# Weighting the experts' rows in their slots and adding them to the residual in the gather itself

## The chip, the cores and the metric

The kernel runs on one core of one Trainium2 chip. The metric is the device time of one execution in microseconds, the median of several runs. A profiled execution also has a span: the time from its first to its last recorded event.

## The reference

The reference is one decoder layer over 8 x 256 = 2048 tokens of width 512: retention, then cross-attention, then a feed-forward with eight experts, each added to a residual. The change lies in the feed-forward alone, in fp32:

```python
xf = layernorm(x)                                   # 2048 x 512
probs = softmax(xf @ gate_w.T)                      # 8 experts
top_p, top_i = top_k(probs, 2)                      # each token goes to two experts
out_e = (silu(xf @ fc1[e].T) * (xf @ fc2[e].T)) @ proj[e].T     # hidden width 352
shared = (silu(xf @ s1.T) * (xf @ s2.T)) @ sproj.T              # hidden width 1408
x = x + top_p[0] * out_e[top_i[0]] + top_p[1] * out_e[top_i[1]] + sigmoid(xf @ sg.T) * shared
```

## The kernel before

The residual `X` stays in SBUF as 16 tiles (`NT`) of 128 tokens by 512 columns. Matrix products are made of three passes over high and low halves of fp32 values (`matmul3`), so TensorE has the most work.

The feed-forward runs in stages. The shared expert goes first, in `STEPS` = 44 steps: 11 pieces of the hidden width, each over 4 groups (`G`) of 512 tokens. Its last eight steps are only half done there; their hidden values are held, and their down products follow at the very end (`held_down`). Meanwhile DVE works out the router: `gain[:, k, t]` is a token's weight for its first (`k` = 0) or second (`k` = 1) expert, `rows[:, k, t]` the row that it has in a table in DRAM. Tokens are sorted by expert into 39 slots (`SLOTS`) of 128 rows. Of a token's two rows, `k` = 0 is the one of the expert with the lower number, so no such row belongs to the last expert.

GpSimd (POOL) writes each token's normalized row to its two places of `rows_in` (`scatter`, 32 indirect DMAs, between its halves of pieces 3 to 6), splits the weights of the shared expert (`split`, pieces up to 10) and of the experts (`fetch` and `expert`).

Then TensorE works through the 39 slots. For each one SP loads 128 rows, TensorE transposes them, multiplies up, transposes the hidden values and multiplies down; ACT copies the product from PSUM to `ye` (`product_out`, three buffers); SP stores `ye` to `rows_out`. Each engine works through its list in the order written.

The end, which the change is about:

- POOL gathers 16 tiles of `k` = 0 rows into `early`, as soon as the last expert but one is through (semaphore `ye_done`); at most three are in flight (`landed0`). Then it waits until all `ye` stores have landed (ACT adds 3 to `ye_done` for this) and gathers 16 tiles of `k` = 1 rows into `late`.
- TensorE runs `held_down(0)` to `held_down(3)`: four sums of 128 x 512 each into PSUM. `held_down(2)` and `(3)` wait until DVE has added the sums of two groups before (`dadded`), whose PSUM banks they reuse. `held_down(3)` also needs two last pairs of hidden values split by ACT and DVE (`pair_high` and `pair_low`, 6 and 7).
- DVE does, in this order: 16 sums with `early` (`expert_sum(t, 0)`), `pair_low(6)` and `(7)`, 16 additions of the shared expert (`dadded`), 16 sums with `late` (`expert_sum(t, 1)`).
- SP stores tile `t` of the residual to the output when `expert_sum(t, 1)` is done.

Of the kernel before, what the change touches and what calls it, by code (L numbers as in the profile page):

```python
# [6 lines left out]
FP32 = mybir.dt.float32  # L7
# [4 lines left out]
ALU = mybir.AluOpType  # L12
# [3 lines left out]
P = 128  # L16
# [64 lines left out]
def retention(nc, X, slots, first, table, x_dram, wa_dram, decay_dram, rot_dram, gn_dram, blk_dram, ident, ident_dram,  # L81
# [4 lines left out]
    with ExitStack() as mem:  # L86
# [86 lines left out]
        def _(sp):  # L173
# [24 lines left out]
            for which in range(2):  # L198
                for g in range(B):
                    sp.dma_start(pack_dram[g, which, 3 * XD:3 * XD + 2, :, :, :].rearrange("r h c (a s) -> (r h c a) s", a=TB),  # L200
                                 fix[:, which, :]).then_inc(fix_out, 16)
            for n in range(SLOTS):
                for rows in row_tables:
                    sp.dma_start(rows[n * P:(n + 1) * P, :], zero_dram).then_inc(filled, 16)
# [13 lines left out]
            sp.wait_ge(fix_out, 32 * B)  # L218
            sp.wait_ge(filled, 32 * SLOTS)

# [1396 lines left out]
def feed_forward(nc, X, final, row_tables, lead, ws_dram, we_dram, ident, out_dram):  # L1617
# [12 lines left out]

    rows_in, rows_out = row_tables
    with ExitStack() as mem:
        def sb(name, shape, dt=FP32, stack=mem):
            return stack.enter_context(nc.sbuf_tensor("c_" + name, shape, dt))

        def pb(name, shape, stack=mem):
            return stack.enter_context(nc.psum_tensor("c_" + name, shape, FP32))
# [7 lines left out]
        with ExitStack() as view:  # L1645
            eraw = sb("eraw", [P, RING, 2 * EW], FP32, view)
        with ExitStack() as view:
            sb("below", [P, 2 * EW], FP32, view)
            late = sb("late", [P, NT, C], FP32, view)
            sb("between", [P, 2 * EW - NT * C], FP32, view)  # L1650
            early = sb("early", [P, NT, C], FP32, view)
        ring = sb("ring", [P, RING * 2 * EW], FP32R)
# [25 lines left out]
        gain = sb("gain", [P, 2, NT])  # L1678
        rows = sb("rows", [P, 2, NT], I32)
        tiles_e, upto, base = sb("tiles_e", [P, E]), sb("upto", [P, E]), sb("base", [P, E])  # L1680
        words = sb("words", [P, 5])
# [3 lines left out]
        with ExitStack() as view:  # L1685
            tp, rl = pb("tp", [P, 2, C], view), pb("rl", [P, C], view)
        with ExitStack() as view:
            eh, ey = pb("eh", [P, C], view), pb("ey", [P, 2, C], view)
# [25 lines left out]
        ye_out = [sem("ye_out%d" % k) for k in range(3)]  # L1714
        landed0, landed1 = [sem("landed0%d" % k) for k in range(3)], [sem("landed1%d" % g) for g in range(G)]
        ph_done, pl_done, pm_done, dm_done, dadded = (sem(k) for k in ("ph_done", "pl_done", "pm_done", "dm_done", "dadded"))
        summed, freed = sem("summed"), sem("ring_freed")
        block = mem.enter_context(nc.Block())
# [22 lines left out]
        def rows_at(n):  # L1741
            return xe[:, n % 4, :]

        def tile_of(idx):
            return 4 * (idx // 4 % G) + idx % 4

        @block.sync
        def _(sp):
# [11 lines left out]
            for f in range(3, HID):  # L1760
                piece(f)
            sp.wait_ge(scattered, 16 * 2 * NT)
            sp.wait_ge(ymm_done, 4 * G * 9)
            for n in range(6):
# [6 lines left out]
            for t in range(NT):  # L1771
                sp.wait_ge(summed, NT + t + 1)
                sp.dma_start(out_dram[:, t, :], X[:, t, :]).then_inc(stored, 16)
# [3 lines left out]
        def _(pool):  # L1777
# [26 lines left out]

            def gather(t, k, into):
                nc.gpsimd.indirect_dma_start(  # L1806
                    out=into[:, t, :], out_offset=None, in_=rows_out,
                    in_offset=bass.IndirectOffsetOnAxis(ap=rows[:, k, t:t + 1], axis=0)).then_inc(landed1[t // 4] if k else landed0[t % 3], 16)

# [17 lines left out]
            for f in range(7, HID):  # L1827
                split(f)
            expert(0)
            pool.wait_ge(fc_done, STEPS)  # L1830
# [14 lines left out]
            for t in range(NT):  # L1845
                if t >= 3:
                    pool.wait_ge(landed0[t % 3], 16 * (t // 3))
                gather(t, 0, early)
            pool.wait_ge(ye_done, SLOTS + 3)
            for t in range(NT):  # L1850
                gather(t, 1, late)

        @block.vector
        def _(dve):
# [187 lines left out]
            for n in range(SLOTS):  # L2042
# [5 lines left out]
                if 2 <= n < 8:  # L2048
                    pair_low(n - 2)
            def expert_sum(t, k):  # L2050
                if k:
                    dve.wait_ge(landed1[t // 4], 64)
                    dve.wait_ge(dadded, t + 1)
                else:
                    dve.wait_ge(landed0[t % 3], 16 * (t // 3 + 1))
                nc.vector.scalar_tensor_tensor(out=X[:, t, :], in0=(early, late)[k][:, t, :], scalar=gain[:, k, t:t + 1],
                                               in1=X[:, t, :], op0=ALU.mult, op1=ALU.add).then_inc(summed, 1)

            for t in range(NT):
                expert_sum(t, 0)  # L2060
            pair_low(6)
            pair_low(7)
            for g in range(G):
                for k in range(4):
                    t = 4 * g + k
                    dve.wait_ge(dm_done, t + 1)
                    dve.wait_ge(summed, t + 1)
                    nc.vector.scalar_tensor_tensor(out=X[:, t, :], in0=sum_at(g, k), scalar=shared[:, t:t + 1],
                                                   in1=X[:, t, :], op0=ALU.mult, op1=ALU.add).then_inc(dadded, 1)
            for t in range(NT):  # L2070
                expert_sum(t, 1)

        @block.scalar
        def _(act):
# [50 lines left out]
            def product_out(n):  # L2125
                act.wait_ge(d_done, n + 2)
                if n >= 3:
                    act.wait_ge(ye_out[n % 3], 16 * (n // 3))
                nc.scalar.copy(ye[:, n % 3, :], ey[:, n % 2, :]).then_inc(ye_done, 1)

# [33 lines left out]
            high_xT(1)  # L2164
            act.wait_ge(hf_done, STEPS)
            expert_silu(0)
            for n in range(SLOTS):
                high_hT(n)
                if n + 1 < SLOTS:
                    expert_silu(n + 1)  # L2170
                if n + 2 < SLOTS:
                    high_xT(n + 2)
                product_out(n)
                if 2 <= n < 8:
                    pair_high(n - 2)
# [7 lines left out]
        def _(pe):  # L2183
# [248 lines left out]
def decoder_layer(nc, ins, out_dram):  # L2432

    with ExitStack() as mem:
        X = mem.enter_context(nc.sbuf_tensor("residual", [P, NT, C], FP32))
        ident = mem.enter_context(nc.sbuf_tensor("identity", [P, P], FP32))
        tables = [nc.dram_tensor("c_rows_" + k, (SLOTS * P, C), FP32).ap() for k in ("in", "out")]
        final = [mem.enter_context(nc.sbuf_tensor("final_" + k, [P, NT], FP32)) for k in ("mean", "var", "rstd")]
# [30 lines left out]
```

## Time and profile before

| | us |
|---|---|
| time, median of 3 runs (1445.61 to 1447.66) | 1446.95 |
| time of the profiled execution | 1445.69 |
| its span | 1443.9 |
| TensorE busy (matmul) | 1332.0 |
| DVE busy | 850.2 |
| GpSimd busy | 515.6 |
| ScalarE busy | 483.9 |

The profiled execution is 1.3 us below the median, and its time is 1.8 us above its span. A busy share is a mean over the whole span; the last 40 us look quite different from the rest, and the change has to be read there.

### The profile page before, as it was taken

What the parts mean: (1) busy time and instruction counts of PE and PEld (TensorE: products, weight loads), DVE (VectorE), ACT (ScalarE), POOL (GpSimd) and SP (SyncE); (2) the same over time, 40 slices, a digit from 0 to 9 for tenths busy, and PEclk for the clock granted to TensorE, in tenths of its full rate; (3) what the DMA queues carried; (4) which work ended last, traced back from release to release, by engine and by line L of the source; (5) the groups of instructions that cost most, each with busy time, mean ns of one, the idle gap of its engine ahead of it and who ended that gap; (6) DMA issues with size and microseconds to landing.
All of it is one profiled execution on the core that took longest, in us unless ns stands there. A gap on an engine that the chain in (4) does not pass through costs nothing. (4 is left out here: it accounts for less than half of the span.)

```text
span 1443.9 us, 24104 instructions
## 1 busy us (share of the span) xinstructions
PE 1332.0 (92%) x8442; PEld 1071.4 (74%) x8442; DVE 850.2 (59%) x1516; ACT 483.9 (34%) x756; POOL 515.6 (36%) x353
## 2 busy tenths in 40 slices
PE   6899999998489999999889999999999999999994
PEld 5577777776366667666557788888887889999983
DVE  5666667675588887788763557556554243222247
ACT  4122222224156556565574311111110233223220
POOL 1122212215354333343142006542133375574045
PEclk9999999999789999999999999999999999999998
DMA  7991000000465445544600002330000434334256
GB/s 252 329 330 59 0 0 0 0 1 23 148 180 164 145 144 156 164 138 143 180 19 22 1 22 99 138 147 22 22 23 30 161 127 151 136 137 149 74 161 232
DMA packets 84891, 159.83 MB, mean 111 GB/s; under 512 B 8560, under 2 KB 61936, under 8 KB 81392
## 3 DMA queue, kind: packets, MB, share of 16 engines
q1 hardware_dynamic: 78544, 124.19, 27.3%
q0 software_dynamic: 6272, 34.61, 6.6%
q8 instruction: 51, 0.84, 0.2%
q14 instruction: 24, 0.20, 0.0%
HBM read 109.22 MB, written 69.47 MB: 124 GB/s over the span
## 5 line engine op out<-in xcount | busy, mean ns | idle before, releaser
L1278 DVE TENSOR_REDUCE b_mx<-b_rt 128x4 f32<-128x1024 f32 x128 | 156.3, 1221 | 51.4 <-PE b_rt L1100 51.3
L1435 ACT ACTIVATE b_pf<-b_rt,b_zero 128x1024 f32<-128x1024 f32 x128 | 142.8, 1116 | 126.7 <-PE b_rt L1112 126.4
L1961 DVE SCALAR_TENSOR_TENSOR residual<-c_yp,c_shared,residual 128x512 f32<-128x512 f32 x144 | 103.8, 744 | 113.6 <-PE c_yp L43 113.6
L41 PE MATMUL c_fc<-c_xh,c_w 128*128 128x512 f32 x352 | 137.7, 391 | 0.0
L43 PE MATMUL c_fc<-c_xh,c_w 128*128 128x512 f32 x352 | 137.1, 389 | 0.0
L42 PE MATMUL c_fc<-c_xl,c_w 128*128 128x512 f32 x352 | 137.0, 389 | 0.0
L41 PE MATMUL c_fc<-c_ring,c_xTl 128*128 x312 | 105.8, 339 | 0.0
L2099 ACT ACTIVATE c_s<-c_fc 128x512 f32<-128x512 f32 x44 | 26.3, 598 | 232.0 <-PE c_fc L43 231.9
L43 PE MATMUL c_fc<-c_ring,c_xTh 128*128 x312 | 100.8, 323 | 0.0
L42 PE MATMUL c_fc<-c_ring,c_xTh 128*128 x312 | 100.6, 322 | 0.0
L1781 POOL TENSOR_TENSOR c_w<-c_wraw,c_zero 128x1536 fp32r<-128x1536 f32 x9 | 24.8, 2751 | 202.5 <-DMA c_wraw<-in_c_ws 108.5
L1975 DVE TENSOR_TENSOR c_hTl<-c_eh,c_hTh 128x384 fp32r<-128x384 f32 x39 | 21.7, 557 | 120.0 <-ACT c_hTh L2123 120.0
L1100 PE MATMUL b_rt<-weights_b 50*128 50x256 f32 x512 | 66.5, 339 | 26.5 <-DVE b_mx L1278 19.7
L1100 PEld LDWEIGHTS b_rt<-weights_b 50*128 50x128 f32 x512 | 39.7, 191 | 60.1 <-DVE b_mx L1278 31.9
L1801 POOL TENSOR_TENSOR c_ring<-c_eraw,c_zero 128x2816 fp32r<-128x2816 f32 (+1 forms) x16 | 62.8, 3926 | 53.2 <-DMA c_eraw<-in_c_we 53.2
L1803 POOL TENSOR_TENSOR c_ring<-c_eraw,c_ring 128x2816 fp32r<-128x2816 f32 (+1 forms) x16 | 78.8, 4926 | 1.3
L43 PEld LDWEIGHTS c_fc<-c_xh,c_w 128*128 128x128 f32 x352 | 66.1, 188 | 13.9
L41 PEld LDWEIGHTS c_fc<-c_xh,c_w 128*128 128x128 f32 x352 | 66.1, 188 | 13.5
L42 PEld LDWEIGHTS c_fc<-c_xl,c_w 128*128 128x128 f32 x352 | 66.1, 188 | 13.3
L1125 PE MATMUL b_av<-b_pf,b_vp 128*32 128x256 f32 x1024 | 69.2, 388 | 0.0
L41 PE MATMUL a_gemm<-weights_a,a_xl 128*128 128x512 f32 x128 | 56.2, 439 | 9.2 <-DVE a_xl L455 9.2
L41 PEld LDWEIGHTS c_fc<-c_ring,c_xTl 128*128 128x128 f32 x312 | 59.0, 189 | 7.4 <-issue 6.7
(386 smaller groups left out, 3499.3 us busy)
## 6 DMA issues: line engine op xcount, KB each, us to landing
weights_b<-b_pack SPq DMA_DIRECT2D x128, 200.0 KB
c_eraw<-in_c_we POOLq DMA_DIRECT2D x8, 2176.0 KB, 9.6
b_pack<-b_hi SPq DMA_DIRECT2D x56, 256.0 KB, 2.5
c_rows_in<-in_b_ctx SPq DMA_DIRECT2D x39, 256.0 KB, 9.9
c_rows_out<-in_b_ctx SPq DMA_DIRECT2D x39, 256.0 KB, 10.0
c_xe<-c_rows_in SPq DMA_DIRECT2D x39, 256.0 KB, 3.0
c_rows_out<-c_ye SPq DMA_DIRECT2D x39, 256.0 KB, 2.0
c_wraw<-in_c_ws SPq DMA_DIRECT2D x11, 768.0 KB, 4.4
```

Of the source, the lines that this page charges most:

```text
L41: nc.tensor.matmul(out, ll, rh, start=start, stop=False)
L42: nc.tensor.matmul(out, lh, rl, start=False, stop=False)
L43: return nc.tensor.matmul(out, lh, rh, start=False, stop=stop)
L1100: last = nc.tensor.matmul(rt[:, e, t * S:(t + 1) * S], qT[r, p, t * P:(t + 1) * P], kT[r, p, :], start=True, stop=True)
L1125: last = nc.tensor.matmul(av[r:r + VW, 0:S], vp[:, j * XH + h, :], pf[:, h % 8, j * S:(j + 1) * S], start=j == 0, stop=j == TB - 1)
L1278: nc.vector.tensor_reduce(out=mx[:, :, 2 * p:2 * p + 2].rearrange("p t e -> p e t"), in_=rt[:, 0:2, :].rearrange("p e (t s) -> p e t s", s ...
L1435: nc.scalar.activation(pf[:, s:s + 2, :], rt[:, 2:4, :], ACT.Exp, scale=XD ** -0.5, bias=zero[:, :]).then_inc(e_done, 1)
L1781: nc.gpsimd.tensor_tensor(w[k][:, 0, :], wraw[k][:, 1, :], zero[:, :].to_broadcast([P, PW]), ALU.add).then_inc(high_done, 1)
L1801: nc.gpsimd.tensor_tensor(high, raw, zero[:, :].to_broadcast([P, hi - lo]), ALU.add).then_inc(high_done, 1)
L1803: nc.gpsimd.tensor_tensor(low, raw, as_f32(high), ALU.subtract).then_inc(ew_done, 1)
L1961: nc.vector.scalar_tensor_tensor(out=X[:, t, :], in0=yp[:, (n * 4 + k) % 3, :], scalar=shared[:, t:t + 1], in1=X[:, t, :], op0=ALU.mult, o ...
L2099: nc.scalar.activation(s[:, n % 2, :], fc[:, n % 2, 0, :], ACT.Silu).then_inc(s_done, 1)
```

## The change

Each expert's rows are multiplied by their token's weight before they are stored, so that what lies in `rows_out` is already weighted. For this the weight has to be known by slot and row. POOL writes `gain` to a new table of one column in DRAM with the indices of the rows (`spread_weights`, 32 indirect DMAs of 128 x 4 bytes, eight after each of the pieces 7 to 10); SP reads the table back as 39 partitions of 128 weights; TensorE transposes it once, ahead of the slots; ACT copies it to SBUF; and `product_out` becomes an activation with a scale for each partition in place of a copy. The transposed weights and the table read back lie in tiles that are no longer used by then.

Both gathers then add their rows to `X` in the DMA (`compute_op=ALU.add`). The 32 sums on DVE and the tiles `early` and `late` are gone. A gather of `k` = 1 into tile `t` waits until DVE has added the shared expert's part of that tile, and that addition waits for the landing of the gather of `k` = 0. SP stores tile `t` when its `k` = 1 gather has landed: the first twelve in groups of four, the last four one by one.

```diff
+            sp.dma_start(row_tables[2].rearrange("(n p) o -> n (p o)", p=P), zero_dram[0:SLOTS, 0:P]).then_inc(filled, 16)
...
+        by_slot = hit[0:SLOTS, :, :].rearrange("p t e -> p (t e)")
+        weight_at = prob[:, :, :].rearrange("p t e -> p (t e)")[:, 0:SLOTS]
...
+        def landing(t):
+            return (landed1[t // 4], 64) if t < NT - 4 else (landed1[G - 1 + t - (NT - 4)], 16)
...
             sp.wait_ge(scattered, 16 * 2 * NT)
+            sp.wait_ge(spread, 16 * 2 * NT)
+            sp.dma_start(by_slot, weights_dram.rearrange("(n p) o -> n (p o)", p=P)).then_inc(weights_in, 16)
             sp.wait_ge(ymm_done, 4 * G * 9)
...
             for t in range(NT):
-                sp.wait_ge(summed, NT + t + 1)
+                sp.wait_ge(*landing(t))
                 sp.dma_start(out_dram[:, t, :], X[:, t, :]).then_inc(stored, 16)
...
+            def spread_weights(t):
+                for k in range(2):
+                    nc.gpsimd.indirect_dma_start(
+                        out=weights_dram, out_offset=bass.IndirectOffsetOnAxis(ap=rows[:, k, t:t + 1], axis=0),
+                        in_=gain[:, k, t:t + 1], in_offset=None).then_inc(spread, 16)
+
+            def gather_add(t, k):
                 nc.gpsimd.indirect_dma_start(
-                    out=into[:, t, :], out_offset=None, in_=rows_out,
-                    in_offset=bass.IndirectOffsetOnAxis(ap=rows[:, k, t:t + 1], axis=0)).then_inc(landed1[t // 4] if k else landed0[t % 3], 16)
+                    out=X[:, t, :], out_offset=None, in_=rows_out,
+                    in_offset=bass.IndirectOffsetOnAxis(ap=rows[:, k, t:t + 1], axis=0),
+                    compute_op=ALU.add).then_inc(landing(t)[0] if k else landed0[t % 3], 16)
...
             for f in range(7, HID):
                 split(f)
+                for t in range(4 * (f - 7), 4 * (f - 6)):
+                    spread_weights(t)
...
             for t in range(NT):
-                gather(t, 1, late)
+                pool.wait_ge(dadded, t + 1)
+                gather_add(t, 1)
...
-            for t in range(NT):
-                expert_sum(t, 0)
-            pair_low(6)
-            pair_low(7)
             for g in range(G):
                 for k in range(4):
                     t = 4 * g + k
                     dve.wait_ge(dm_done, t + 1)
-                    dve.wait_ge(summed, t + 1)
+                    dve.wait_ge(landed0[t % 3], 16 * (t // 3 + 1))
                     nc.vector.scalar_tensor_tensor(out=X[:, t, :], in0=sum_at(g, k), scalar=shared[:, t:t + 1],
                                                    in1=X[:, t, :], op0=ALU.mult, op1=ALU.add).then_inc(dadded, 1)
-            for t in range(NT):
-                expert_sum(t, 1)
+                if g == 0:
+                    pair_low(6)
+                    pair_low(7)
...
-                nc.scalar.copy(ye[:, n % 3, :], ey[:, n % 2, :]).then_inc(ye_done, 1)
+                nc.scalar.activation(ye[:, n % 3, :], ey[:, n % 2, :], ACT.Identity, scale=weight_at[:, n:n + 1],
+                                     bias=zero[:, :]).then_inc(ye_done, 1)
...
             act.wait_ge(hf_done, STEPS)
+            act.wait_ge(turned_done, 1)
+            nc.scalar.copy(weight_at, turned[:, :]).then_inc(weights_done, 1)
             expert_silu(0)
+            act.wait_ge(weights_done, 1)
...
+            pe.wait_ge(weights_in, 16)
+            nc.tensor.transpose(turned[:, :], by_slot, ident[0:SLOTS, 0:SLOTS]).then_inc(turned_done, 1)
             transpose_rows(0)
```

## Rows read from the trace of the kernel before

**Rows 1.** The page, part 1: TensorE's busy time and share.
```profile
PE 1332.0 (92%) x8442; PEld 1071.4 (74%) x8442; DVE 850.2 (59%) x1516; ACT 483.9 (34%) x756; POOL 515.6 (36%) x353
```

**Rows 2.** The chain that ended last, from 1402 us: start us, us, what.
```profile
1402.66 0.60 ACT c_ye L2129
1403.28 2.73 DMA c_rows_out<-c_ye
...
1406.38 6.26 POOL c_late L1806
...
1430.92 6.41 DMA c_late<-c_rows_out,c_rows
```

**Rows 3.** Timeline of POOL: start us, us, instruction, idle time before and its releaser.
```profile
1380.11 1.04 POOL L1806 DMA_INDIRECT c_early<-c_rows_out,c_rows  x1 [53.95 <-ACT c_ye L2129]
...
1384.31 0.95 POOL L1806 DMA_INDIRECT c_early<-c_rows_out,c_rows  x1 [0.65 <-DMA c_early<-c_rows_out,c_rows]
...
1401.38 1.44 POOL L1806 DMA_INDIRECT c_early<-c_rows_out,c_rows  x1 [0.49 <-DMA c_early<-c_rows_out,c_rows]
1403.12 1.02 POOL L1806 DMA_INDIRECT c_early<-c_rows_out,c_rows  x1 [0.30 <-issue]
...
1412.94 0.94 POOL L1806 DMA_INDIRECT c_late<-c_rows_out,c_rows  x1 [0.30 <-issue]
...
1426.72 1.24 POOL L1806 DMA_INDIRECT c_late<-c_rows_out,c_rows  x1 [0.30 <-issue]
```

**Rows 4.** Timeline of DVE from 1399 us.
```profile
1399.90 10.71 DVE L2056 SCALAR_TENSOR_TENSOR residual<-c_early,c_gain,residual 128x512 f32<-128x512 f32 x16
...
1411.74 2.71 DVE L2068 SCALAR_TENSOR_TENSOR residual<-c_fc,c_shared,residual 128x512 f32<-128x512 f32 x4
...
1426.40 8.03 DVE L2056 SCALAR_TENSOR_TENSOR residual<-c_late,c_gain,residual 128x512 f32<-128x512 f32 x12
1437.35 2.74 DVE L2056 SCALAR_TENSOR_TENSOR residual<-c_late,c_gain,residual 128x512 f32<-128x512 f32 x4 [2.91 <-DMA c_late<-c_rows_out,c_rows]
```

**Rows 5.** Timeline of SP's DMA queue: the output's stores.
```profile
1427.17 13.48 SPq L1773 DMA_DIRECT2D out<-residual  x16
```

**Rows 6.** DMA, 1413 to 1427 us: GB/s by slices of 0.35 us, the queue, landings.
```profile
GB/s 12 211 257 234 129 140 269 222 141 152 257 222 141 187 293 164 117 234 281 164 222 222 222 164 316 222 164 129 304 211 140 140 328 211 140 234 211 164 234 293
...
q0 software_dynamic: 854, 2.84, 70.4%
...
c_late<-c_rows_out,c_rows POOLq DMA_INDIRECT x12, 3.7
```

**Rows 7.** DMA, 1427 to 1443.9 us: packets, MB, share of 16 engines.
```profile
q1 hardware_dynamic: 2304, 4.20, 64.5%
q0 software_dynamic: 426, 1.36, 24.5%
```

**Rows 8.** Groups of ACT, shapes apart: count, busy us, mean ns, idle before.
```profile
L2129 ACT COPY c_ye<-c_ey 128x512 f32<-128x512 f32 x39 | 22.9, 588 | 64.5 <-PE c_ey L43 64.5
...
L708 ACT ACTIVATE a_gcn<-a_rt,a_gb,a_ga 128x256 f32<-128x256 f32 x32 | 15.5, 565 | 30.3 <-DVE a_gb L562 30.3
L686 ACT COPY a_qk<-a_gemm 128x256 f32<-128x256 f32 x32 | 11.9, 373 | 128.6 <-PE a_gemm L43 128.6
```

**Rows 9.** POOL's other DMAs: duration min/median/max ns, first and last start us.
```profile
L1787 POOL DMA_INDIRECT c_rows_in<-c_xn,c_rows x32: 957/963/1432, 880.8 to 955.5; - x32
...
L1792 POOL DMA_DIRECT2D c_eraw<-in_c_we x8: 556/562/592, 958.5 to 1298.8; - x8
```

**Rows 10.** Timeline of POOL: the split of piece 10.
```profile
1073.19 3.51 POOL L1783 TENSOR_TENSOR c_w<-c_wraw,c_w 128x1536 fp32r<-128x1536 f32 x1
```

**Rows 11.** Timeline of SP's DMA queue: the first loads of slots' rows.
```profile
1100.20 35.63 SPq L1757 DMA_DIRECT2D c_xe<-c_rows_in  x6
```

**Rows 12.** Timeline of TensorE: matmuls of the held products.
```profile
1414.51 0.50 PE L41 MATMUL c_fc<-c_w,c_keep_low 128*128 128x512 f32 x1 [1.00 <-DVE residual L2068]
...
1425.31 0.39 PE L43 MATMUL c_ex<-c_w 128*128 128x512 f32 x1
```

More of the change, by code:

```diff
@@ L201, in _ @@
                                  fix[:, which, :]).then_inc(fix_out, 16)
+            sp.dma_start(row_tables[2].rearrange("(n p) o -> n (p o)", p=P), zero_dram[0:SLOTS, 0:P]).then_inc(filled, 16)
             for n in range(SLOTS):
-                for rows in row_tables:
+                for rows in row_tables[0:2]:
                     sp.dma_start(rows[n * P:(n + 1) * P, :], zero_dram).then_inc(filled, 16)
@@ L218, in _ @@
             sp.wait_ge(fix_out, 32 * B)
-            sp.wait_ge(filled, 32 * SLOTS)
+            sp.wait_ge(filled, 32 * SLOTS + 16)
         @block.tensor
@@ L1629, in feed_forward @@
     MAGIC = 1.5 * 2.0 ** 23
-    rows_in, rows_out = row_tables
+    rows_in, rows_out, weights_dram = row_tables
     with ExitStack() as mem:
@@ L1646, in feed_forward @@
             eraw = sb("eraw", [P, RING, 2 * EW], FP32, view)
[L1647 to L1651, printed above, removed]
         ring = sb("ring", [P, RING * 2 * EW], FP32R)
@@ L1686, in feed_forward @@
             tp, rl = pb("tp", [P, 2, C], view), pb("rl", [P, C], view)
+        with ExitStack() as view:
+            turned = pb("turned", [P, SLOTS], view)
         with ExitStack() as view:
@@ L1714, in feed_forward @@
         ye_out = [sem("ye_out%d" % k) for k in range(3)]
-        landed0, landed1 = [sem("landed0%d" % k) for k in range(3)], [sem("landed1%d" % g) for g in range(G)]
+        landed0, landed1 = [sem("landed0%d" % k) for k in range(3)], [sem("landed1%d" % g) for g in range(G + 3)]
         ph_done, pl_done, pm_done, dm_done, dadded = (sem(k) for k in ("ph_done", "pl_done", "pm_done", "dm_done", "dadded"))
-        summed, freed = sem("summed"), sem("ring_freed")
+        spread, weights_in, turned_done, weights_done = sem("spread"), sem("weights_in"), sem("turned_done"), sem("weights_done")
+        freed = sem("ring_freed")
         block = mem.enter_context(nc.Block())
@@ L1803, in expert @@
                     nc.gpsimd.tensor_tensor(low, raw, as_f32(high), ALU.subtract).then_inc(ew_done, 1)
-            def gather(t, k, into):
+            def spread_weights(t):
[4 more added lines that the diff above has]
+            def gather_add(t, k):
                 nc.gpsimd.indirect_dma_start(
-                    out=into[:, t, :], out_offset=None, in_=rows_out,
-                    in_offset=bass.IndirectOffsetOnAxis(ap=rows[:, k, t:t + 1], axis=0)).then_inc(landed1[t // 4] if k else landed0[t % 3], 16)
+                    out=X[:, t, :], out_offset=None, in_=rows_out,
+                    in_offset=bass.IndirectOffsetOnAxis(ap=rows[:, k, t:t + 1], axis=0),
+                    compute_op=ALU.add).then_inc(landing(t)[0] if k else landed0[t % 3], 16)
             nc.gpsimd.memset(zero[:, :], 0.0).then_inc(presets, 1)
@@ L1847, in _ @@
                     pool.wait_ge(landed0[t % 3], 16 * (t // 3))
-                gather(t, 0, early)
+                gather_add(t, 0)
             pool.wait_ge(ye_done, SLOTS + 3)
             for t in range(NT):
-                gather(t, 1, late)
+                pool.wait_ge(dadded, t + 1)
+                gather_add(t, 1)
         @block.vector
@@ L2049, in _ @@
                     pair_low(n - 2)
[L2050 to L2057, printed above, removed]
-            for t in range(NT):
-                expert_sum(t, 0)
-            pair_low(6)
-            pair_low(7)
             for g in range(G):
@@ L2436, in decoder_layer @@
         ident = mem.enter_context(nc.sbuf_tensor("identity", [P, P], FP32))
-        tables = [nc.dram_tensor("c_rows_" + k, (SLOTS * P, C), FP32).ap() for k in ("in", "out")]
+        tables = [nc.dram_tensor("c_rows_" + k, (SLOTS * P, wide), FP32).ap() for k, wide in (("in", C), ("out", C), ("weight", 1))]
         final = [mem.enter_context(nc.sbuf_tensor("final_" + k, [P, NT], FP32)) for k in ("mean", "var", "rstd")]
```

## The prediction, made blind

> **What bounds the kernel now.** Over the span TensorE is busy for 1332.0 of 1443.9 us [rows 1], but that ends before the stretch that matters. The chain of waits shows what sets the end. Its last product of the slots is copied by ACT at 1402.66, its store lands 2.73 us after its issue at 1403.28, and from 1406.38 the chain is POOL's 16 late gathers, one after another, until 1430.92; then comes the last landing (6.41) and DVE's last sums [rows 2]. So the last 37.5 us are a tail with POOL, the DMA engines and, for a few us, DVE in turn.
>
> Three things are to be seen in that tail. POOL issues a gather every 1.25 us (1412.94 to 1426.72 is 11 gathers, 1.25 each) [rows 3], but its first late gather lasts 6.26 in place of 0.95 [rows 2]. DVE does two sets of 16 sums of 0.67, 10.71 and 10.77 us [rows 4]; only the last four, 2.74 us, stand behind the last landing. And SP can start the 16 stores of the output only at 1427.17 [rows 5], because DVE does the late sums last; from there the DMA engines are 89% busy (64.5 and 24.5%) [rows 7], after some 14 us at 70.4% [rows 6].
>
> What a DMA costs its engines follows from these. Gathers alone: 2.84 MB are 10.8 tiles of 0.262 MB in 70.4% of 14 us, 0.91 us a tile [rows 6]. Beside the stores: 1.36 MB are 5.2 tiles in 24.5% of 16.9 us, 0.80 a tile; a store: 64.5% of 16.9 over 16, 0.68 [rows 7].
>
> **The change part by part.**
>
> *The weights' way to the slots.* 32 indirect DMAs on POOL, eight behind each piece. Scatters of the same 128 rows take 0.96 [rows 9] and 1.27 with the gap before the next, so eight are 10.2 us. The last eight would follow the split that ends at 1076.7 [rows 10] and end at 1086.9; POOL's conversion of the first expert follows, and slides by 10.2 us; the slots start only near 1135, where the sixth load of rows goes out behind TensorE's first transposes (1100.20 + 35.63) [rows 11]. On SP the wait for `spread` and one 20 KB load stand before the loads of slots' rows, which start at 1100.20 because they wait for TensorE; the spread has landed by about 1090 and the load by about 1093. Cover left: 7 us. Cost 0; if the small writes were slow enough to use up the cover, the loads have another 30 us before TensorE needs the first. The transpose on TensorE and ACT's copy are one instruction each, at most 0.3 us together.
>
> *`product_out` with a scale.* The trace has no such activation from PSUM at 512 columns. At 256 columns one with a scale and bias for each partition takes 565 ns and a copy 373 [rows 8]; I add these 0.19 us to the 588. 37 of 39 hide under TensorE, on an ACT that is 34% busy [rows 1]. The last two don't: the one of slot 37 stands ahead of the cast of the last hidden values, the one of slot 38 is in the chain. Cost 0.4 us, between 0 and 0.5.
>
> *The long first late gather.* It is POOL's 57th DMA of the kernel (32 scatters, 8 fetches, 16 early gathers) [rows 3, 9], and nothing moved during it. Two explanations, and by both it goes from this place. One is bookkeeping that comes due after so many DMAs; with 32 more ahead of it, the 57th falls among the spreads, where POOL has idle time. The other is DVE: its sums read two SBUF operands without a pause from 1399.90 until it turns to PSUM at 1411.74, and the gather ends 0.9 us later [rows 4]. But gathers at 1401.38, 1403.12 and 1426.72 ran in 1.44, 1.02 and 1.24 beside the same sums [rows 3, 4], so I hold the first for likelier. The Trainium skill ("SBUF — State Buffer", the box on the "DVE blocks DMA" trap) says that GpSimd can't write descriptors while DVE holds the shared port; these three gathers speak against it as the whole story, and by it too the stall would go. Gain on POOL: 6.26 less 0.95, 5.3 us, the late gathers starting at 1406.8. It could be as low as 0, if adds bring the stall back in among the late gathers.
>
> *The late gathers as adds.* Nothing in the trace adds in a DMA. A gather reads a row in DRAM and writes it in SBUF; an add also has to read the row in SBUF. Lower bound 0.80 us of the engines' time for a tile (that read costs nothing). A store is a tile's read from SBUF (and a write), 0.68, so read and gather one after the other are 1.48. Upper bound twice the gather alone, 1.82. I take 1.48, the only one built of what must be moved. The Trainium skill ("Collectives: The Full Stack", why ReduceScatter is half of AllGather) has adds limited by their two source reads, at 32.35 against 62.28 GB/s: by that estimate 0.91 becomes 1.75.
>
> *DVE's sums.* 32 sums go, 21.5 us. Sixteen of them only delayed the shared additions. DVE now does these right behind TensorE's products, and TensorE's wait of 1.0 goes: it ends at 1424.7 in place of 1425.7, and as its 48 matmuls from 1414.51 take 0.70 for each sum [rows 12], tile 12 is ready at about 1423.5. On POOL alone the late gathers would then start their last at 1423.5 + 3 x 1.25 = 1427.3. What matters more is that the stores need no DVE any more: they start when the first four tiles have landed, near 1415, and share the engines with the gathers.
>
> *The sum.* Moving starts 0.7 us after the first late gather has been issued (1412.64, and data within 0.7) [rows 2, 6], so at 1406.8 + 0.95 + 0.7 = 1408.5. From there the engines have 16 adds, and 13 or so of the stores before the last gather is through: 16 x 1.48 + 13 x 0.68 = 32.5, to 1441.0. They stay busy: four adds take 5.9 us, until 1414.4, and the next tiles are ready by then. The last landing is seen 0.7 later. Behind it stands one store; in the trace it is 3.8 us from DVE's last sum (1437.35 + 2.74 = 1440.1) to the end [rows 4]. 1441.0 + 0.7 + 3.8 = 1445.5, against 1443.9: 1.6 us longer. The profiled execution goes from 1445.7 to 1447.3; its median stands 1.3 above it, so I say 1448.5 us for 1446.95. In short, the end is 1421.8 + 16c, where c is the cost of an add: equal at 1.38, 0.2% (2.9 us, about what this measurement can tell from no change) faster at 1.20, 0.2% slower at 1.56. The gain of the stall and of early stores is real, and adds in the DMA hand it back.
>
> *The early gathers as adds.* They are held at three in flight. Now a landing is 4.2 us from the start of its gather (1380.11 to 1384.31) [rows 3]; with 0.6 more each three take 4.8, so one every 1.6, and the last of 16 starts at 1404.1. This still fits ahead of 1406.8, by little: from a pitch of 1.7 on it is late, and the late gathers with it. They also share the engines with the last stores of `ye`, whose 2.73 is in the chain; up to 1 us, which I keep for the range.
>
> **The rivals.**
>
> *A. The add is nearly free for the engines* (c up to 1.2). For it: reading and writing SBUF may overlap, and mixed with stores the gather came down from 0.91 to 0.80 already. Against: the read is real traffic. At c = 0.80 POOL's order binds: last gather at 1427.3, landing 3.8 later as now [rows 6], store 3.8: 1434.9, 9 us less. At 1.1: 1439.4. Middle of the case 1438.5, so a time of 1441.5 us.
>
> *B. POOL writes more for an add, and becomes the bound.* 0.95 us for 128 rows may become up to 1.9 if it works for each row that is read, a pitch of 2.2. The 32 gathers then run back to back from 1380.11: last start 1380.1 + 31p, landing about 5.1 later, store 3.8. It decides from p = 1.84 on; at 2.0 the end is 1451, at 2.2 it is 1457. Against: the direct DMAs, each of one expert's weights, take only 0.57, so not all of it goes with the amount [rows 9]. Time 1454 us.
>
> *C. The add costs twice a gather or more* (c from 1.6). By what the page on collectives has, 1.75, the end is 1449.8; the stall's return among the late gathers has the same effect, up to 5.3. Time 1453 us.
>
> **How the numbers follow.** The forecast (c between 1.2 and 1.56, POOL not the bound) has 0.40, and its own range is 1444 to 1451; A has 0.31, B 0.17, C 0.12. Faster is A with a little of the forecast's edge, 0.32; the same is most of the forecast, 0.30; slower is B, C and the forecast's upper part, 0.38. For eight in ten the range goes from 1439 (all but the lowest part of A) to 1457 (B up to a pitch of about 2.1).
>
> **What would show it.** The first late gather on POOL at about 0.95; one POOL indirect DMA of some 6 us among the spreads before 1090, if the count is its cause. The mean time of POOL's adds tells B (1.3 or more). The share of the engines times the window over the tiles moved gives c. Output stores should begin near 1415 and spread over 27 us; the last late gather should be issued near 1427 and land some 10 us later, behind queued work. TensorE should end near 1425. If the engines are less than 90% busy from 1415 to 1440, the sum is wrong in kind; if the early gathers' last start is after 1407, the whole tail moves by that.

## Result and the profile after

The changed kernel takes 1453.67 us (median of 12 runs, 1450.43 to 1464.69) against 1447.07 for the one before (12 runs, 1445.09 to 1448.28). The ratio is 1.0054, with an interval of 1.0036 to 1.0073: slower by 0.54%. Its profiled execution took 1452.04 us with a span of 1450.2, against 1445.69 and 1443.9.

The page of the changed kernel, part 1. Against [rows 1] DVE is 24 us less busy, POOL 44 us more.
```profile
PE 1331.2 (92%) x8443; PEld 1071.2 (74%) x8443; DVE 826.5 (57%) x1484; ACT 491.4 (34%) x757; POOL 559.5 (39%) x385
```

POOL from 1377 us to its last instruction, from its timeline: start, us, engine, line, operation, and in brackets the idle time before it and what ended it.
```profile
1377.87 1.68 POOL L1819 DMA_INDIRECT residual<-c_rows_out,c_rows  x1 [53.65 <-ACT c_ye L2134]
1379.86 1.56 POOL L1819 DMA_INDIRECT residual<-c_rows_out,c_rows  x1 [0.30 <-issue]
...
1387.88 1.53 POOL L1819 DMA_INDIRECT residual<-c_rows_out,c_rows  x1 [0.94 <-DMA residual<-c_rows_out,c_rows]
...
1402.41 1.54 POOL L1819 DMA_INDIRECT residual<-c_rows_out,c_rows  x1 [1.36 <-DMA residual<-c_rows_out,c_rows]
...
1408.16 1.54 POOL L1819 DMA_INDIRECT residual<-c_rows_out,c_rows  x1 [0.50 <-DMA residual<-c_rows_out,c_rows]
1410.01 1.54 POOL L1819 DMA_INDIRECT residual<-c_rows_out,c_rows  x1 [0.31 <-issue]
...
1437.71 1.54 POOL L1819 DMA_INDIRECT residual<-c_rows_out,c_rows  x1 [0.30 <-issue]
```
The 16 early adds start from 1377.87 to 1408.16, the 16 late ones from 1410.01 to 1437.71. An add occupies POOL for 1.54 us where a gather took 0.95 [rows 3], and the next starts 1.84 after it at the soonest, where that was 1.25. The long gather of 6.26 us [rows 2] is gone. But the first late add starts right behind the last early one: POOL has 32 adds in one queue and waits, beyond the 0.30 between any two, for some 2.5 us in all.

The chain of waits that ended last, after TensorE's and DVE's last work in it.
```profile
1420.27 0.76 DVE residual L2072
1421.08 1.56 POOL residual L1819
1422.63 0.30 issue
1422.94 1.55 POOL residual L1819
1424.49 1.84 POOLq L1633
...
1437.71 1.54 POOL residual L1819
```
Where DVE's late sums once stood behind the last landing, there is now POOL alone. The wait for DVE at 1421.08 ended when POOL's own queue did (0.30 idle before that add, as before every other), so it cost nothing.

One line of the code, ACT's `product_out`; then SP's 16 stores of the output, from SP's timeline.
```profile
L2134 ACT ACTIVATE c_ye<-c_ey,c_zero,c_prob x39: 777/779/782, 1145.8 to 1400.5; 128x512 f32<-128x512 f32 x39
```
```profile
1421.12 24.90 SPq L1780 DMA_DIRECT2D out<-residual  x16
```
The stores begin 6 us earlier than in [rows 5], but end later, at 1446.0.

Windows: us, busy time of PE, PEld, DVE, ACT and POOL, granted clock, DMA share, GB/s.
```profile
1382.00:1400.00 18.00, 16.21 (x92) 14.34 (x91) 3.62 (x7) 4.99 (x9) 14.03 (x10) 1.00 0.97 169
1408.00:1427.00 19.00, 14.27 (x63) 11.47 (x62) 8.54 (x13) 0.00 (x0) 15.79 (x11) 0.93 0.96 163
1427.00:1448.00 21.00, 0.00 (x0) 0.00 (x0) 0.00 (x0) 0.00 (x0) 10.42 (x7) 0.50 1.09 278
```
The DMA traffic from 1415 to 1440: queue, packets, MB, share of the 16 engines; then the issues with their time to landing.
```profile
q0 software_dynamic: 1832, 3.34, 80.5%
q1 hardware_dynamic: 1152, 2.10, 23.6%
issues: line engine op xcount, KB each, median us to landing
out<-residual SPq DMA_DIRECT2D x11, 256.0 KB, 6.4
residual<-c_rows_out,c_rows POOLq DMA_INDIRECT x14, 7.2
```
3.34 MB are 12.7 tiles in 80.5% of 25 us, so an add occupies the DMA engines for 1.58 us, where a gather took 0.91 alone and 0.80 beside stores. From 1382 to 1405 it is 1.72:
```profile
q0 software_dynamic: 1625, 2.95, 84.2%
```
The two queues' shares from 1415 to 1440 add up to 104%: packets of the two overlap there, so 1.58 is the time of an add's packets and may hold some waiting beside the stores. The engines are busy for 94% or more from 1382 on, but until the stores begin they move little, 169 GB/s from 1382 to 1400 and 136 from 1408 to 1421.

**The tail in three legs.** The last product of the slots is copied by ACT at different times in different executions: 1402.66 before, 1400.54 after, though `product_out` is longer now. From 1140 to 1170 the granted clock was 0.96 before and 1.00 after. So kernels are compared here from that copy on: (1) from the copy to the first late gather, (2) from there to the start of the last one, (3) from there to the end of the span. The starts are read from the timelines of POOL and ACT.

| kernel | leg 1 | leg 2 | leg 3 | tail |
|---|---|---|---|---|
| before | 3.7 | 24.5 | 13.0 | 41.2 |
| after | 9.5 | 27.7 | 12.5 | 49.7 |

8.4 us more: 5.8 in leg 1, 3.2 in leg 2, and 0.5 less in leg 3.

Leg 1 holds two things. ACT's first instruction behind the landing of the last `ye` store shows when that landing was seen, first before, then after:
```profile
1406.18 0.62 ACT L2157 CAST c_w<-c_keep 128x512 fp32r<-128x512 f32 x1 [2.93 <-DMA c_rows_out<-c_ye]
1406.23 0.62 ACT L2163 CAST c_w<-c_keep 128x512 fp32r<-128x512 f32 x1 [4.91 <-DMA c_rows_out<-c_ye]
```
It is 3.5 us behind the copy before and 5.7 after, and before the change the first late gather started 0.2 behind it. So of the 5.8 us some 2.2 are the store, which lands later beside the early adds, and some 3.6 are adds that POOL still had in front of it.

One profile shows one execution. The changed kernel's second profile has legs of 9.0, 27.7 and 12.3; but two profiles of the kernel of experiment 1 have tails of 37.8 and 35.1, and the kernel before with nothing changed in the tail (experiment 4) has 44.9. In the two kernels profiled twice, legs 1 and 3 repeat within 0.7 us and leg 2 within 2.4. So a tail that differs by less than some 4 us in one profile of each kernel shows little by itself.

### The profile page after: what moved, and what is told of

It reads as the page before. It is cut to its first block and busy times, and to the rows that moved or that the text cites. A ratio compares the mean times of both kernels' runs of the same rounds, so it can differ in the third digit from the quotient of the medians.

```text
span 1450.2 us, 24095 instructions
## 1 busy us (share of the span) xinstructions
PE 1331.2 (92%) x8443; PEld 1071.2 (74%) x8443; DVE 826.5 (57%) x1484; ACT 491.4 (34%) x757; POOL 559.5 (39%) x385
## 5 line engine op out<-in xcount | busy, mean ns | idle before, releaser
L1101 PEld LDWEIGHTS b_rt<-weights_b 50*128 50x128 f32 x512 | 39.6, 191 | 59.8 <-DVE b_mx L1279 31.9
L43 PEld LDWEIGHTS c_fc<-c_xh,c_w 128*128 128x128 f32 x352 | 66.1, 188 | 13.7
L1819 POOL DMA_INDIRECT residual<-c_rows_out,c_rows x32 | 49.4, 1545 | 65.6 <-ACT c_ye L2134 53.6
```

Source lines behind the costliest of these rows:

```text
L43: return nc.tensor.matmul(out, lh, rh, start=False, stop=stop)
L1101: last = nc.tensor.matmul(rt[:, e, t * S:(t + 1) * S], qT[r, p, t * P:(t + 1) * P], kT[r, p, :], start=True, stop=True)
L1819: nc.gpsimd.indirect_dma_start(out=X[:, t, :], out_offset=None, in_=rows_out, in_offset=bass.IndirectOffsetOnAxis(ap=rows[:, k, t:t + 1], ...
```

## Experiments

They ran in three groups, each on one chip together with the kernel before. In the first and the third, the kernel before itself varied, from 1445 to 1462 us (medians 1454.08 and 1453.18); in the second it was at 1445.80 (1443.61 to 1450.71). Its slower executions have the lower mean granted clock: in the third group 0.968 to 0.974 in the seven above 1458 us, 0.974 to 0.978 in the eight below 1450. A longer tail lowers that mean by itself (0.50 from 1427 on, where TensorE is idle), so which of the two is the cause stays open. So times are given as ratios to the kernel before beside them, and the legs say in which stretch a difference lies.

**1. Does the adding cost it?** The changed kernel, twice, without the addition in the DMA: the rows then overwrite the residual, and its output lacks what lay there.

```diff
-                    compute_op=ALU.add).then_inc(...)
+                    ).then_inc(...)
```


> The changed kernel with both gathers as plain writes into the residual's tiles, all waits kept; the output lacks the residual and the first experts' rows, its time is what counts. Theory (the add is what costs): POOL's gathers fall from 1.54 to 0.95 us, their pitch from 1.84 to 1.25, the engines' time for a tile from about 1.65 to 0.8 to 0.9, the last late gather starts near 1425 where it started at 1437.7, and the time is 1436 to 1440 us, some 9 below the kernel before. Rival (the order of the waits costs: each late gather behind its shared addition, stores behind groups of four): POOL still sits idle between gathers for more than 0.3 us, and the time stays at 1447 or more.

> The changed kernel once more, as the measure for the two runs beside it on one chip. From its first measurement: a ratio to the kernel before of 1.004 to 1.007; in the profile POOL's adds at 1.54 us, pitch 1.84, the last late gather about 37 us behind the last copy of ye, and the whole tail from that copy to the end 47 to 50 us.

> The changed kernel with plain gathers again (the output lacks the residual and the first experts' rows), now beside the changed kernel on one chip. If the add is the cost: 8 to 12 us below the changed kernel. If most of what was seen in the first run came from the state of that chip, 3 us or less.

First run: 1446.69, ratio 0.9952 (0.9929 to 0.9974). In the second group the changed kernel took 1451.48, ratio 1.0040 (1.0025 to 1.0055), and the one without the addition 1438.67, ratio 0.9944 (0.9931 to 0.9957). So the adding costs 12.8 us (medians of 6 and 5 executions), and without it the change would have gained 7. The traffic of the latter from 1410 to 1430:
```profile
q0 software_dynamic: 1101, 3.62, 59.8%
q1 hardware_dynamic: 1178, 2.15, 28.5%
```
3.62 MB are 13.8 tiles in 59.8% of 20 us: 0.87 us a tile. The changed kernel had 1.63 in this group, from 1416 to 1444:
```profile
q0 software_dynamic: 2024, 3.69, 82.0%
```
The Trainium skill ("Collectives: The Full Stack", why ReduceScatter is half of AllGather) says of a collective's add that it is limited by its two source reads, with a measured ratio of 1.93; here it is 1.63 / 0.87 = 1.87, so the size agrees, while no run here shows the reads themselves.

**2. POOL's pace or the DMA engines' work?** The same kernel without addition, but POOL clears 600 columns of an unused buffer behind each late gather, so that it goes at nearly the pace of adds.

```diff
                 gather_add(t, 1)
+                nc.gpsimd.memset(eraw[:, t // 8, t % 8 * 600:t % 8 * 600 + 600], 0.0)
```


> The plain gathers of the run before, but POOL fills 600 columns of a free tile with zeros, 0.5 to 0.6 us, behind every late gather: POOL's pace of the add (1.84) without its work on the DMA engines. The output lacks the same parts. If POOL's pace is the cost of the late adds, the last late gather starts where it does with adds and the time is 2 to 5 us below the changed kernel, 6 to 9 above the plain gathers. If the DMA engines' work is the cost, the stores fill in and the time is within 3 us of the plain gathers.

1443.60, ratio 0.9985 (0.9974 to 0.9995). POOL's timeline shows the pace, 1.73 us:
```profile
1419.13 0.95 POOL L1819 DMA_INDIRECT residual<-c_rows_out,c_rows  x1 [0.16 <-issue]
1420.08 0.62 POOL L1868 MEMSET c_eraw<- 128x600 f32 x1
1420.86 0.95 POOL L1819 DMA_INDIRECT residual<-c_rows_out,c_rows  x1 [0.16 <-issue]
```
4.9 of the 12.8 us are back with the DMA engines no busier than without the addition (0.87 us a tile in this run too). The other 7.9 us don't come back: the early gathers are as quick here as without the addition, and the adding's load on the DMA engines is gone. The legs of the second group:

| kernel | leg 1 | leg 2 | leg 3 | tail |
|---|---|---|---|---|
| no addition | 4.9 | 19.6 | 10.6 | 35.1 |
| no addition, slow issue | 4.9 | 26.0 | 10.4 | 41.3 |
| changed kernel | 9.0 | 27.7 | 12.3 | 49.1 |

The changed kernel's leg 2 is 15 starts at POOL's own pitch (15 x 1.84 = 27.6). So of 14.0 us in the tail, 8.1 lie in the late adds at POOL's pace, 4.1 in what comes before them, and 1.7 behind the last one. These are single executions. The other profiles of the two kernels (5.6, 22.0 and 10.3 without the addition, 9.5, 27.7 and 12.5 with it) give 5.7, 3.9 and 2.2 for the same three.

What a quicker POOL would gain with adds was not run, and it may be little: the DMA engines are nearly full as well. By the prediction's formula for them, 1421.8 + 16c, adds of 1.63 end at 1447.9, a tail of 45.2 us; with the first late add 5.3 us later, as measured, that is 50.5, an estimate, against 49.7 and 49.1 measured. So POOL's pace is enough to explain leg 2, and the DMA engines' work would nearly be enough as well.

**3. Does POOL's time go with the bytes?** The table of results and both gathers have 256 columns in place of 512, so half the residual gets no expert's part.

```diff
-                    out=X[:, t, :], out_offset=None, in_=rows_out,
+                    out=X[:, t, 0:C // 2], out_offset=None, in_=rows_out,
```


> The changed kernel, but the table of the experts' rows has 256 columns: half rows are stored and added, the right half of the experts' part is left out of the output. POOL handles as many rows, the DMA engines move half. Theory (POOL's 1.54 us for 128 added rows sets the pace of the late gathers): the pitch stays at 1.84, the last late gather still starts at 1435 to 1438, and only what stands behind it gets shorter: 1444 to 1448 us. Rival (the DMA engines set the pace): the gathers follow faster or the tail shrinks by half of their extra work, about 13 us: 1438 to 1441 us.

1448.39, ratio 0.9958 (0.9938 to 0.9979). POOL's timeline and the traffic from 1420 to 1446:
```profile
1441.39 1.54 POOL L1819 DMA_INDIRECT residual<-c_rows_out,c_rows  x1 [0.30 <-issue]
1443.23 1.54 POOL L1819 DMA_INDIRECT residual<-c_rows_out,c_rows  x1 [0.30 <-issue]
1445.08 1.54 POOL L1819 DMA_INDIRECT residual<-c_rows_out,c_rows  x1 [0.30 <-issue]
```
```profile
q0 software_dynamic: 1977, 1.80, 48.9%
```
POOL's price stays at 1.54 us for 128 rows: it doesn't go with their width. The DMA engines' price falls to 0.93 us (13.7 half tiles of 0.131 MB in 48.9% of 26 us). The legs are 7.3, 27.7 and 10.2: against the changed kernel above, leg 1 and leg 3 are shorter by 1.8 and 2.1, leg 2 is the same. Halving the engines' work doesn't touch the late adds' pace. It quickens the early ones, which wait less for landings (1.87 from start to start, where the changed kernel of the second group had 2.05).

**4. What made the long gather?** Two kernels. The first is the kernel before with the 32 writes of weights added, and the weights not used: the 57th DMA of POOL then lies among these writes. The second is the kernel before with DVE's early sums set between the shared additions, so that DVE turns to PSUM between any two of them.

```diff
                 split(f)
+                for t in range(4 * (f - 7), 4 * (f - 6)):
+                    spread_weights(t)
```


> The kernel before plus only the 32 indirect DMAs that write the weights by slot (the table is not used). If the 6.3 us gather is due because 56 DMAs of POOL's have gone before it, it now lies among the spreads and the first late gather takes 0.95: 1441 to 1442 us. If it comes from DVE's 18 back-to-back operations on two SBUF operands, it stays where it is and the time is the same as before, 1446 to 1448. Either way nothing before 1135 us moves.

```diff
-            for t in range(NT):
-                expert_sum(t, 0)
...
                     t = 4 * g + k
+                    expert_sum(t, 0)
                     dve.wait_ge(dm_done, t + 1)
```


> The kernel before with DVE's list alone reordered: each early sum stands directly ahead of the shared addition of its tile, as in the changed kernel's order, and the late sums stay last. If DVE's back-to-back sums of two SBUF operands hold up POOL, the first late gather takes 0.95 to 2 us, the last starts near 1425.5 where it started at 1430.9, and DVE's late sums become the end (16 x 0.67 behind 1426): 1441 to 1443 us. If the count of DMAs is the cause, the gather of 6.3 us stays and the time is within 1 us of the kernel before.

With the writes: 1450.64, ratio 0.9986 (0.9959 to 1.0013). The long gather is there still, though it is now POOL's 89th DMA. POOL's timeline, then DVE's:
```profile
1409.42 5.53 POOL L1814 DMA_INDIRECT c_late<-c_rows_out,c_rows  x1 [9.94 <-ACTq L2188]
1415.25 0.95 POOL L1814 DMA_INDIRECT c_late<-c_rows_out,c_rows  x1 [0.30 <-issue]
```
```profile
1402.24 10.68 DVE L2066 SCALAR_TENSOR_TENSOR residual<-c_early,c_gain,residual 128x512 f32<-128x512 f32 x16
...
1413.45 0.68 DVE L2023 TENSOR_TENSOR c_w<-c_wraw,c_w 128x512 fp32r<-128x512 f32 x1
1414.05 2.71 DVE L2078 SCALAR_TENSOR_TENSOR residual<-c_fc,c_shared,residual 128x512 f32<-128x512 f32 x4
```
It ends at 1414.95, again 0.9 us after DVE's first operation with an operand from PSUM, as in [rows 4]. The count is refuted. The legs of this profile are 3.0, 23.4 and 18.5: DVE's shared additions of the last group begin at 1432.19, though TensorE's last matmul began at 1427.80, and no run explains that pause.

With DVE's other order: 1449.41, ratio 0.9965 (0.9942 to 0.9988). POOL's timeline, then DVE's:
```profile
1410.76 0.95 POOL L1806 DMA_INDIRECT c_late<-c_rows_out,c_rows  x1 [6.85 <-ACTq L2178]
1412.01 1.40 POOL L1806 DMA_INDIRECT c_late<-c_rows_out,c_rows  x1 [0.30 <-issue]
```
```profile
1435.45 0.75 DVE L2065 SCALAR_TENSOR_TENSOR residual<-c_ex,c_shared,residual 128x512 f32<-128x512 f32 x1
1436.12 10.68 DVE L2056 SCALAR_TENSOR_TENSOR residual<-c_late,c_gain,residual 128x512 f32<-128x512 f32 x16
```
No stall, as the explanation by DVE's sums has it, and the last late gather starts 24.2 us behind the copy in place of 28.3. But the tail is 41.8 us: DVE has the rows early and sums them last, 10.7 us in one piece. In this profile the stall's 5 us are taken up by DVE's order. Beside the varying kernel before, its median is 4.7 us lower, about what was expected, but its tail isn't shorter: what the stall alone is worth stays open.

**5. The order of DVE and SP alone, without the change.** Weights are applied on DVE as before; the late sums of four tiles follow each group's shared additions, and the last four tiles get a semaphore each. In the first kernel early sums and shared additions alternate; in the second nine early sums go first and seven behind the first group.

```diff
+            for t in range(9):
+                expert_sum(t, 0)
+            shared_part(0)
+            pair_low(6)
+            pair_low(7)
+            for t in range(9, NT):
+                expert_sum(t, 0)
+            for g in range(1, G):
+                shared_part(g)
+                for t in range(4 * (g - 1), 4 * g):
+                    expert_sum(t, 1)
...
```


> The kernel before, no adds in the DMA and no weighting in the slots: DVE's list is reordered so that the early sum stands ahead of the shared addition of its tile and the late sums of a group follow the next group, and SP stores each tile then. Theory (what was there to gain lay in DVE's order: no 6.3 us gather, stores beside the gathers): the late gathers end near 1426, DVE has 48 sums of 0.67 from 1404 on and ends at 1436 to 1438: 1440 to 1443 us, 0.2 to 0.45% below the kernel before. Rival (TensorE then waits for DVE's additions, which stand behind late sums that wait for landings): 1446 or more.

> The reordered kernel before (no adds in the DMA), with DVE's list in blocks: nine early sums while TensorE is still at the last slot, the shared additions of group 0, pair_low, seven early sums, then shared additions and late sums by groups. Theory (the first reordering had DVE idle 5.5 us and then bound to the end): DVE works without a pause from 1400, 50 operations of 0.68 end at 1434, and the end is 3.8 us later: a tail of 35 to 36 us behind the last copy of ye where the kernel before has 41.2, a time 4 to 6 us below it. If blocks of seven early sums hold POOL up again: a gather of 3 us or more in the profile and less than 3 us gained.

Alternating: 1446.58, ratio 1.0010 (0.9994 to 1.0026); legs 4.9, 21.9, 14.8. DVE is idle for 5.5 us before TensorE's first held sum, then it is the bound until 1439.5. In blocks: 1446.85, ratio 0.9944 (0.9919 to 0.9970); legs 4.9, 22.6, 9.7, a tail of 37.1 against 41.2 before. POOL's timeline there has two gathers of middle length, at 1420.82 and here; both begin among late sums of DVE with two SBUF operands (1419.74 to 1422.39 and 1425.03 to 1427.68) and end 0.9 us after DVE turns to PSUM, as the long ones do.
```profile
1424.86 0.95 POOL L1809 DMA_INDIRECT c_late<-c_rows_out,c_rows  x1 [0.31 <-issue]
1426.11 2.47 POOL L1809 DMA_INDIRECT c_late<-c_rows_out,c_rows  x1 [0.30 <-issue]
```
So the order in blocks alone is 0.56% faster than the kernel before, as much as the changed kernel without its addition (0.56%, in another group), with no sum taken from DVE. That the gain lies in the tail rests on one profile of each.

**6. Adds in one half only.** The first kernel adds early rows in the DMA and gathers late ones plainly, for DVE to add in blocks; the second does the reverse; the third adds the first 8 early tiles in the DMA and leaves 24 sums to DVE. All have the weighted rows.

```diff
-                gather_add(t, 0)
+                gather_add(t, 0) if t < 8 else gather_early(t)
...
-                gather_add(t, 1)
+                gather_late(t)
```


> The changed kernel with adds in the DMA for the early gathers alone; the late ones are plain and DVE adds their rows (16 sums). If the late adds are what costs: pitch of the late gathers 1.25, the last one near 1428 (the early adds still delay the first to 7 to 8 us behind the last copy of ye), tail 36 us, 4 to 6 us below the kernel before. If the early adds cost as much: no gain against the kernel before, within 2 us.

> The changed kernel with adds in the DMA for the late gathers alone; the early ones are plain and DVE adds their rows, in blocks. If the late adds are the cost, about 4 us of the changed kernel's loss go (the late gathers start 4 us behind the last copy of ye, not 8) and it stays as slow as or slower than the kernel before: 0 to 3 us above it. If the early adds were the cost, it is 4 us or more below the kernel before.

> Adds in the DMA for early tiles 0 to 7 alone, everything else plain and summed on DVE in blocks. POOL's early gathers then take 25 us and are through before the last ye has landed, DVE has 8 sums fewer than in the reordering in blocks. If POOL and DVE are the bounds as read so far, the late gathers run from 4 us behind the last copy of ye at 1.25, and the tail is 31 to 33 us, 8 to 10 us below the kernel before. Rival: it does no better than the reordering in blocks, because the landing of the last late gather ends both.

| adds in the DMA | time | ratio (interval) | legs | tail |
|---|---|---|---|---|
| early 16 | 1445.14 | 0.9938 (0.9914 to 0.9962) | 10.4, 19.0, 12.3 | 41.6 |
| late 16 | 1454.16 | 1.0004 (0.9982 to 1.0026) | 5.2, 28.7, 12.4 | 46.2 |
| first 8 | 1442.60 | 0.9926 (0.9901 to 0.9951) | 5.5, 20.8, 10.9 | 37.2 |
| none (blocks) | 1446.85 | 0.9944 (0.9919 to 0.9970) | 4.9, 22.6, 9.7 | 37.1 |

All four ran in one group. Early adds lengthen leg 1 by 5 us, late adds leg 2 by some 6. With eight early adds POOL is through in time for the slots' end:
```profile
1393.95 1.54 POOL L1824 DMA_INDIRECT residual<-c_rows_out,c_rows  x1 [0.38 <-DMA residual<-c_rows_out,c_rows]
1396.09 0.99 POOL L1830 DMA_INDIRECT c_early<-c_rows_out,c_rows  x1 [0.61 <-DMA residual<-c_rows_out,c_rows]
...
1407.84 0.95 POOL L1830 DMA_INDIRECT c_early<-c_rows_out,c_rows  x1 [0.30 <-issue]
1409.09 1.20 POOL L1835 DMA_INDIRECT c_late<-c_rows_out,c_rows  x1 [0.30 <-issue]
```
It has the lowest ratio of all, 0.74% below the kernel before, but its tail is that of the kernel with no add at all, as its rival had it, and the intervals of the two overlap: that the eight adds help is not shown. The 16 early adds are 0.62% faster by the ratio with a tail no shorter than before, which the legs don't explain. In that kernel DVE stood idle for 2.5 us, 1.8 of them with its rows landed, and for 2.7 us with TensorE done long before; pauses of this kind came in at least three of the kernels, and no run explains them.

## Why the prediction was right in its direction and too low in its size

The forecast was 1448.5 us in a range of 1439 to 1457, with slower the likeliest of the three outcomes at 0.38. It came out at 1453.67, inside the range, on the side of rivals B and C. So the direction was right by a small margin: the forecast's own case, at 0.40 and up to 1451, had a rise of 1.6 us, less than it held for measurable, and had the DMA engines alone set the end. The 6.6 us came by what B and C name, 0.29 together. Step by step:

- **The weights' way, 0 us: right.** The first load of slots' rows went out at 1099.69, against 1100.20 [rows 11], and the 32 writes took 0.96 each. The cover was thinner than reckoned: the weights' load went out at 1096.47 and not by 1093, since a write landed up to 11.1 us after its issue. The timeline has one instruction more on TensorE (0.25 us) and one on ACT (0.20).
- **`product_out`, +0.19 each: right.** 0.78 against 0.59. The Trainium skill ("ScalarE: Activation LUTs", What ACT_TABLE_LOAD costs) has 93 ns for each operand read by partition, and two of them, 186 ns, are nearly this difference.
- **The stall goes: right, by the explanation held less likely.** None of the writes took more than 1.3 us, and experiment 4 refutes the count. It goes with DVE's unbroken run of operations with two SBUF operands. The Trainium skill ("SBUF — State Buffer", Two separate sides) lets such an operation lock out a GpSimd operation that reads SBUF for the whole instruction. The trace agrees that there is a stall, but it lasted through more than one instruction, and neighbours beside the same sums passed in 0.95 to 1.44.
- **"One every 1.6, and the last of 16 starts at 1404.1": wrong, and this step cost most.** It costed the early adds by the landing alone, 4.2 us plus 0.6, with three in flight. The start-to-start time was 2.02: POOL needs 1.84 at the least, and the landing takes 5.9. The last early add started at 1408.16, the first late one at 1410.01, 9.5 us behind the last copy where the forecast had 4.1. The prediction had named this as what would shift the whole tail. 5.3 us; of these some 1.8 would have come without a backlog on POOL, since the last `ye` store was seen to land 5.7 behind the copy (it had put up to 1 us for this into the range and none into the sum).
- **POOL at 1.25 a gather: wrong by half.** It is 1.84, exactly where rival B was said to begin to decide. The nearest row for an add was the plain gather; the argument against B (direct DMAs take 0.57) said nothing on a second operand for each row. Experiment 2 prices this pace (1.73 there) at 4.9 us of time, on the late gathers alone and with the DMA engines unloaded.
- **c = 1.48: too low.** 1.58 to 1.72, inside the bounds of 0.80 and 1.82. By the formula 1421.8 + 16c it is 1.6 to 3.8 us. But the formula doesn't describe the late adds: POOL sent them at its own pitch from the first to the last, and the engines' extra work appears in early landings (leg 1) and in the last ones, of up to 8.0 us. From the first late add to the last landing the sum had 34.9 us, and it was 1437.7 + 8.0 - 1410.0 = 35.7, so the length came out near by another way. The estimate of 1.75, from the Trainium skill ("Collectives: The Full Stack", why ReduceScatter is half of AllGather), is nearer to the 1.72 of the early adds; for the late ones, at 1.58, the 1.48 is.
- **Last store, 3.8: 4.5** (1450.2 - 1445.7), and **stores from 1415**: they began at 1421.1, since four adds have to land, each some 7 us after its start.

The forecast's tail was 1445.5 - 1402.7 = 42.8, the measured one 49.7. The difference of 6.9 is 5.3 for the late start, 0.8 for the late leg and 0.7 for the last store; the slots ended 2.1 earlier in this execution, which leaves the 4.7 us by which the span was missed. Rival B, POOL at a pitch of 1.84 to 2.0 with its 32 gathers back to back, is what happened: from the first to the last it is 1.93 on the mean, for which B's own sum gives 1448.8. Rival C came with it, with a landing of 8.0 where B had 5.1. A is refuted.

Open: under which condition a GpSimd gather stalls beside DVE's sums, since gathers of 0.95, 1.2, 1.4, 2.5 and 5.5 us all occurred beside them; DVE's pauses with its data there; how much of the early adds' delay is POOL's pace and how much the engines' landing (half rows take 1.8 us off leg 1, but their last `ye` store is halved too); and why the kernel before varies by 15 to 17 us in two of the groups.

## What to carry to other kernels

An addition in the DMA is not a copy with a sum for free: price it on the engine that issues it and on the DMA engines. In the tail, where both are busy, it cost 12.8 us; with eight early adds, where POOL has idle time, neither a cost nor a gain was shown. Before an engine is relieved, look at the order of its work: here DVE's late sums standing behind all others, and the stores behind them, were a loss of their own, and a new order alone made the kernel 0.56% faster. When a queue of N equal instructions takes a dearer form, multiply over the whole queue, from its first start to the next consumer, not only over the part in the chain.

## What the runs showed of the hardware that was not expected

- An indirect DMA that adds occupies POOL for 1.54 us for 128 rows in place of 0.95, at 512 columns and at 256 alike.
- By the time of its packets it occupies the DMA engines for 1.58 to 1.72 us for 256 KB in place of 0.87, and in the records it has 144 packets a tile (1832 packets for 12.7 tiles) in place of 80 (1101 for 13.8).
- A plain gather was held 5.5 and 6.3 us while DVE ran 16 sums of two SBUF operands, and ended 0.9 us after DVE's first operation on PSUM; two of 2.47 us in the kernel with blocks ended in the same way. Beside early sums that alternate with additions from PSUM, many gathers took 1.2 us and none was held longer than 1.4. The adds took 2.1 at most, also beside DVE's early sums in the kernel with late adds alone.
